# A patch-and-text transformer block on one core: stationary values, 32-row score tiles, a mask written by TensorE, and a nine-step pipe in attention

## The chip, the cores and the metric

One core of one Trainium2 chip runs the whole program. The metric is device time in microseconds (us), lower is better; the median of a few runs is compared. The core has five instruction queues: PE (TensorE, matrix products), DVE (VectorE), ACT (ScalarE), POOL (GpSimd) and SP (SyncE, which here only issues DMAs). Each runs its own instructions in program order, and they wait for each other through semaphores.

## What is computed

```python
h = tok(x)                             # 32 x 36 patches of 768: layernorm, @ Wp + bp, layernorm
h = concatenate([h, txt], axis=1)      # 32 sequences of T = 113 rows, D = 256
h = h + attn(layernorm(h))
h = h + ffn(layernorm(h))              # blockwise FP4 of inputs and weights, SwiGLU, inner width 704
# attn(x):
q = (x @ Wq.T).reshape(B, T, 16, 16); k = (x @ Wk.T).reshape(B, T, 16, 16)
v = (x @ Wv.T).reshape(B, T, 8, 32)
q = rotary(rmsnorm(q)) / 4; k = rotary(rmsnorm(k))      # per head of 16
attn = softmax(where(causal, q @ k.T, -inf))            # 16 score heads
attn = attn[:, :, 0] - lam * attn[:, :, 1]              # pairs of them
out = layernorm(attn @ v) * (1 - LAMBDA_INIT)           # per head of 32
return out.reshape(B, T, 256) @ Wproj.T
```

## The kernel before

The program has three stages. The front makes the patch tokens, nine tiles of 128 rows (`front(i)`), quantises the weights of the last stage piece by piece and prepares the attention weights; it writes tokens to `h_dram`. The attention stage works on one sequence at a time: `attention(b)` is one pass of a software pipe, in which each engine does different steps of several sequences (the number ahead of a step in the lists called `steps` is added to b: `(2, qk)` makes the queries and keys of sequence b + 2). The feed-forward stage (FFN) works on 29 tiles of 128 rows. All three are written for five engines at once by `pipeline`, which interleaves the last front steps with the first passes and the last passes with the first FFN steps; the middle passes are a hardware loop. The order on each engine is written by hand; only semaphores tie the engines.

What one pass does, for the sequences in flight: SP loads the rows `hx` (two DMAs, patch rows and text rows), DVE takes their moments (`ln_sums`), ACT takes Ln and Exp of all variances of the pass together (`roots`, tile `var`), DVE refines them (`newton_step`) and normalises (`ln_apply`, tile `xn`). PE transposes, ACT and DVE split the result into a high and a low half (`xo_hi`, `xo_lo`), and PE multiplies by the weights in three products (`split3`, line L138). `scale_qk`, `cosines`, `sines` (on POOL) and `rope_sum` apply the norm and the rotation; the four tiles of that are all called `rope` in the trace. PE transposes them; ACT writes the keys (`k_t`) and the queries in blocks (`q_blk`), of which four slots share 64 rows. PE makes four groups of scores, ACT exponentiates each, POOL zeroes the later keys in each (`mask`), and PE multiplies: the probabilities are the stationary operand, the values with a column of ones (33 columns) the moving one, once for each of 16 heads. DVE mixes the pairs (`mix`: L931 to L942), and another norm, the transposes, the output product (`project`) and the residual (L967, with rows loaded again as `hr`) follow. Stores go to `h2_dram`. `bank_a` holds both the transposes (`xo_ps`) and the output product, so the transposes of the next pass wait for the residual.

```python
def residual(b):
    dve.wait_ge(m["proj_made"], b - 1)
    dve.wait_ge(m["hr_loaded"], 32 * b - 32)
...
run(b, seq, (
    (3, ln_sums), (-1, mix), (1, rope_sum), (-2, residual),
    (2, qk_sums), (-1, z_sums), (-2, out_sums), (-1, z_var), (2, qk_var),
    ((3, -2), variances)))
```

## Time and profile before

| | |
|---|---|
| time, median of 3 runs | 660.13 us (658.75 to 660.4) |
| time of the profiled execution | 662.52 us |
| its span | 660.8 us |
| PE busy | 576.4 us (87%) |
| DVE busy | 554.1 us (84%) |
| ACT busy | 322.1 us (49%) |
| POOL busy | 309.8 us (47%) |
| granted TensorE clock, mean | 0.948 |

The span runs from the first to the last instruction. A busy share is an average over three stages, so it says little by itself; what a pass of the loop costs is read from the timelines of the engines. A mean of one of the costliest groups (L741, the product with the values) is 262 ns for each of 1024 instructions, but matmuls overlap, so their cost is read from the distance between starts.

### The profile page before, as it was taken

What the parts mean: (1) busy time and instruction counts of PE and PEld (TensorE: products, weight loads), DVE (VectorE), ACT (ScalarE), POOL (GpSimd) and SP (SyncE); (2) the same over time, 40 slices, a digit from 0 to 9 for tenths busy, and PEclk for the clock granted to TensorE, in tenths of its full rate; (3) what the DMA queues carried; (4) which work ended last, traced back from release to release, by engine and by line L of the source; (5) the groups of instructions that cost most, each with busy time, mean ns of one, the idle gap of its engine ahead of it and who ended that gap; (6) DMA issues with size and microseconds to landing.
All of it is one profiled execution on the core that took longest, in us unless ns stands there. A gap on an engine that the chain in (4) does not pass through costs nothing. (4 is left out here: it accounts for less than half of the span.)

```text
span 660.8 us, 14226 instructions
## 1 busy us (share of the span) xinstructions
PE 576.4 (87%) x3666; PEld 470.0 (71%) x3666; DVE 554.1 (84%) x1444; ACT 322.1 (49%) x760; POOL 309.8 (47%) x455
## 2 busy tenths in 40 slices
PE   5665568999999999999999998589999999999996
PEld 4554455767776776777677676478888888888885
DVE  5999847898889889888988985498888888888884
ACT  2242215655665665566565564244544444445442
POOL 2455523555455445545554553155455445545542
PEclk9878776999999999999999997789999999999999
DMA  6900000011111111111111101111111111111111
GB/s 173 325 17 23 24 16 18 27 38 41 30 40 35 35 35 38 40 34 37 35 41 29 42 23 46 30 39 49 48 54 52 54 48 54 49 48 48 57 32 35
DMA packets 33734, 31.99 MB, mean 48 GB/s; under 512 B 6098, under 2 KB 32050, under 8 KB 33714
## 3 DMA queue, kind: packets, MB, share of 16 engines
q1 hardware_dynamic: 33714, 31.75, 16.3%
q8 instruction: 9, 0.15, 0.1%
q14 instruction: 11, 0.09, 0.0%
HBM read 23.02 MB, written 8.71 MB: 48 GB/s over the span
## 5 line engine op out<-in xcount | busy, mean ns | idle before, releaser
L741 PE MATMUL bank<-v_sb,pt 113*113 113x33 f32 x1024 | 109.1, 262 | 0.0
L741 PEld LDWEIGHTS bank<-v_sb,pt 113*113 113x113 f32 x1024 | 108.4, 181 | 0.7 <-issue 0.7
L858 POOL TENSOR_SCALAR_AFFINE_SELECT pt<-pt 113x452 f32<-113x452 f32 x128 | 73.9, 600 | 68.5 <-ACT pt L798 68.5
L798 ACT ACTIVATE pt<-bank 113x452 f32<-113x452 f32 x128 | 63.1, 545 | 38.2 <-PE bank L729 38.2
L138 PE MATMUL bank<-wgu_hi,fx_hi 128*128 128x512 f32 x174 | 69.5, 399 | 8.0 <-DVE fx_lo L1131 8.0
L1177 POOL TENSOR_TENSOR h_deq<-fh,fhb 128x704 f32<-128x704 f32 x29 | 40.3, 1389 | 68.8 <-DVE fhb L1084 56.3
L729 PE MATMUL bank<-q_blk,k_t 64*113 64x452 f32 x256 | 67.7, 605 | 0.0
L138 PE MATMUL bank<-wgu_hi,fx_lo 128*128 128x512 f32 x174 | 66.8, 384 | 0.0
L138 PE MATMUL bank<-wgu_lo,fx_hi 128*128 128x512 f32 x174 | 66.7, 384 | 0.0
L138 PE MATMUL bank<-wqkv_hi,xo_hi 128*113 128x256 f32 (+1 forms) x128 | 50.3, 393 | 17.7 <-DVE xo_lo L923 17.7
L1191 POOL TENSOR_TENSOR fh<-fh,fhb 128x704 f32<-128x704 f32 x29 | 40.3, 1391 | 42.2 <-DVE fhb L1145 42.2
L138 PE MATMUL bank_a<-wd_hi,fh_hi 128*128 128x256 f32 x174 | 54.4, 313 | 2.4 <-DVE fh_lo L1088 2.4
L138 PEld LDWEIGHTS bank<-wqkv_hi,xo_hi 128*113 128x113 f32 x128 | 23.5, 183 | 43.0 <-issue 34.2
L867 POOL COPY v_sb<-v_next 113x256 f32<-113x256 f32 x32 | 12.8, 401 | 87.0 <-PE bank L741 63.8
L850 POOL TENSOR_TENSOR rope<-rope,trig 113x256 f32<-113x256 f32 x64 | 46.4, 744 | 13.1 <-DVE rope L905 13.1
L138 PE MATMUL bank_a<-wd_lo,fh_hi 128*128 128x256 f32 x174 | 49.1, 282 | 0.0
L138 PE MATMUL bank_a<-wd_hi,fh_lo 128*128 128x256 f32 x174 | 49.0, 282 | 0.0
L1243 ACT ACTIVATE bank_b<-fx 128x256 fp32r<-128x256 f32 x29 | 11.3, 388 | 76.2 <-POOL fx L1184 75.1
L809 ACT ACTIVATE q_blk<-bank_b,slot_rows 128x226 f32<-128x226 f32 x128 | 46.4, 445 | 0.0
L138 PE MATMUL bank<-wqkv_lo,xo_hi 128*113 128x256 f32 (+1 forms) x128 | 45.0, 352 | 0.0
L138 PE MATMUL bank<-wqkv_hi,xo_lo 128*113 128x256 f32 (+1 forms) x128 | 44.7, 350 | 0.0
L138 PEld LDWEIGHTS bank<-wgu_hi,fx_hi 128*128 128x128 f32 x174 | 33.8, 194 | 14.2 <-DVE fx_lo L1131 5.6
(160 smaller groups left out, 1531.3 us busy)
## 6 DMA issues: line engine op xcount, KB each, us to landing
xb<-h_dram SPq DMA_DIRECT2D x29, 129.0 KB, 2.1
rb<-h_dram SPq DMA_DIRECT2D x29, 128.0 KB, 2.0
h_dram<-h SPq DMA_DIRECT2D x32, 112.9 KB
out<-res SPq DMA_DIRECT2D x28, 128.0 KB, 1.7
px<-in_patches SPq DMA_DIRECT2D x9, 384.0 KB, 10.1
hx<-in_txt SPq DMA_DIRECT2D x32, 77.0 KB
hr<-in_txt SPq DMA_DIRECT2D x32, 77.0 KB
wf<-in_wgu SPq DMA_DIRECT2D x1, 1408.0 KB, 8.0
```

What stands on the lines that cost most here:

```text
L138: last = pe.matmul(dst, a(k), w(k), start=(start and n == 0), stop=(n == len(passes) - 1))
L729: pe.matmul(sc_ps[g % 2][0:T, :], k_t[rows, c, :], q_blk[rows, c, :, :].rearrange("p s t -> p (s t)"), start=True, stop=True).then_inc(m[" ...
L741: mm = pe.matmul(pv_ps[s % 2][0:T, s // 2, :], pt[0:T, s, :], v_sb[0:T, s // 2, :], start=True, stop=True, skip_group_check=True)
L798: act.activation(pt[0:T, GS * g:GS * (g + 1), :].rearrange("p s t -> p (s t)"), sc_ps[g % 2][0:T, :], ACT.Exp, scale=1.0 / math.sqrt(HD)). ...
L809: i = act.activation(q_blk[:, :, s, :], qkt_ps[:, 0:KD, :], ACT.Copy, scale=slot_rows[:, s:s + 1])
L850: pool.tensor_tensor(dst[:, :, half, :], src[:, :, 1 - half, :], table, ALU.mult).then_inc(m["qk_sin"], 1)
L858: pool.affine_select(out=grp, in_=grp, compare_op=ALU.is_ge, fill=0.0, base=0, pattern=[[0, GS], [1, T]], channel_multiplier=-1).then_inc( ...
L867: pool.tensor_copy(v_sb[0:T, :, 0:VD], blocks(v_next[0:T, :], VD)).then_inc(m["v_moved"], 1)
L1177: pool.tensor_tensor(blocks(h_deq[:, 0:INTER], BLK), blocks(h_code[:], BLK), spread(h_scale[:], BLK), ALU.mult).then_inc(f["h_deq"], 1)
L1191: pool.tensor_tensor(blocks(h_quot[:], BLK), blocks(hid[:], BLK), spread(h_inv[:], BLK), ALU.mult).then_inc(f["h_quot"], 1)
L1243: act.activation(x_abs.bitcast(F32R), x_quot[:], ACT.Abs, scale=STEP).then_inc(f["x_abs"], 1)
```

## The change

- Scores: a tile has 32 rows (two slots) in place of 64, so four tiles lie one under the other; each has its own bank. `scores` writes the causal mask into each bank first (identity times a table of 0 and -32768, both bfloat16), and eight products of 226 columns add to it. POOL's `mask` is gone.
- Values: `pv` keeps a head's values stationary (32 columns) and moves the probabilities of the pair (226 columns), four heads at four column positions. The result is transposed, so ACT copies it (`ot_copy`) and PE turns it back (`pv_transposes`). A rotation of each head's values by a zero-sum basis, made in the front, leaves 31 columns; the 32nd carries the sum of the probabilities. It also carries the epsilon of the norm of the output, so `eps0` and `z_var` are gone.
- Norm: the attention weights are centred in the front (`turn_values`, `average_attention`, `turn_projection` on PE, `centre_attention` and `attn_low` on DVE), so `hx` is transposed as it is, `ln_apply` is gone, the values take the norm's factor in `v_stage`, and the rmsnorm takes it as its epsilon (`epsilons`, POOL).
- `rope_sum` moves from DVE to POOL.
- The pipe has nine steps: passes -4 to 35 in place of -3 to 34. The residual is three passes behind (`(-3, residual)`), the store four; `xo_hi`, `xo_lo`, `rstd` and `v_sb` have two buffers; the loop body holds two passes.

```diff
-ROW = P // 2
+ROW = P // NG
...
+MASKED = -2.0 ** 15
...
+            def centre_attention(_):
+                dve.wait_ge(k["wqkv_averaged"], 1)
+                for cols, mean in ((slice(0, 2 * D), bank_a[:]), (slice(2 * D, 3 * D), bank_b[:, 0:D])):
+                    w = wqkv_raw[:, :, cols]
+                    dve.tensor_tensor(w, w, mean.unsqueeze(1).broadcast_to(list(w.shape)),
+                                      ALU.subtract).then_inc(k["wqkv_centred"], 1)
...
-            def v_subtract(_):
...
-            def attn_low(c):
-                pool.wait_ge(k["attn_high"], 2)
-                pool.tensor_tensor(wqkv_lo[:, c, :], wqkv_raw[:, c, :], wqkv_hi[:, c, :].bitcast(F32),
-                                   ALU.subtract).then_inc(k["attn_low"], 1)
...
+            def turn_values(_):
...
+            def average_attention(_):
+                pe.wait_ge(k["wv_copied"], 1)
+                pe.wait_ge(k["bias_ready"], 1)
+                for cols, mean in ((slice(0, 2 * D), bank_a[:]), (slice(2 * D, 3 * D), bank_b[:, 0:D])):
+                    for c in range(KD):
+                        mm = pe.matmul(mean, average_d[:], wqkv_raw[:, c, cols], start=(c == 0), stop=(c == KD - 1))
+                mm.then_inc(k["wqkv_averaged"], 1)
+            def turn_projection(_):
...
-                if seq(b, 3):
-                    after(sp, m["ln_applied"], b + 3)
-                    load_rows(hx, b + 3, m["hx_loaded"])
-                if seq(b, -3):
-                    sp.wait_ge(m["h2_ready"], b - 2)
-                    sp.dma_start(h2_dram[bass.ds((b - 3) * T, T - 1), :], h2[0:T - 1, :]).then_inc(m["h2_stored"], 16)
-                    sp.dma_start(h2_dram[bass.ds((b - 3) * T + T - 1, 1), :], h2[T - 1:T, :]).then_inc(m["h2_stored"], 16)
-                if seq(b, -1):
-                    after(sp, m["h2_added"], b - 1)
-                    load_rows(hr, b - 1, m["hr_loaded"])
...
+            def load(s, _):
...
+                after(sp, m["ln_stats"], s)
+                after(sp, m["xo_made"], s)
+                load_rows(sp, hx, s, m["hx_loaded"])
+            def load_residual(s, _):
+                after(sp, m["h2_added"], s)
+                load_rows(sp, hr, s, m["hr_loaded"])
...
+                run_order(b, odd, one, ((-4, store), (-2, load_residual), (4, load)))
...
-            def transposes(b):
-                after(pe, m["h2_added"], b - 2)
-                if seq(b, 2):
-                    pe.wait_ge(m["ln_applied"], b + 3)
-                    for k in range(KD):
...
+            def transposes(s, odd):
+                after(pe, m["h2_added"], s - OD)
+                after(pe, m["xo_low"], s)
...
-            def scores(b, g):
...
+            def scores(s, odd):
...
+                pe.wait_ge(m["q_blocked"], s + 1)
+                pe.wait_ge(m["kt_copied"], s + 1)
+                after(pe, m["exp_made"], NG * s)
+                after(pe, m["ot_copied"], s)
+                for r in range(NG):
+                    pe.matmul(sc_ps[r][0:T, :], ident_16[0:T, 0:T], mask_16[0:T, :], start=True, stop=True)
+                for c in range(KD):
+                    for r in range(NG):
+                        rows = slice(r * ROW, (r + 1) * ROW)
+                        mm = pe.matmul(sc_ps[r][0:T, c * SLOTS * T:(c + 1) * SLOTS * T], k_t[rows, c, :],
+                                       q_blk[rows, c, :, :].rearrange("p s t -> p (s t)"),
+                                       start=False, stop=True, skip_group_check=True)
+                        if c == KD - 1:
+                            mm.then_inc(m["scores_made"], 1)
...
+            def pv(s, odd):
+                pe.wait_ge(m["exp_made"], NG * s + NG)
+                pe.wait_ge(m["v_staged"], s + 1)
+                for c in range(KD):
+                    for r in range(NG):
+                        mm = pe.matmul(ot_ps[r * VD:(r + 1) * VD, c, :, :].rearrange("p s t -> p (s t)"),
+                                       v_sb[odd][0:T, c * NG + r, :],
+                                       pt[0:T, r, c * SLOTS:(c + 1) * SLOTS, :].rearrange("p s t -> p (s t)"),
+                                       start=True, stop=True, skip_group_check=True)
...
+            def pv_transposes(s, odd):
+                pe.wait_ge(m["ot_copied"], s + 1)
+                after(pe, m["mix_step"], 4 * s)
+                after(pe, m["v_staged"], min(NSEQ, s + 3) if isinstance(s, int) else s + 3)
+                for i in range(2):
+                    for c in range(KD):
+                        mm = pe.transpose(o_ps[0:T, i, c, :], ot_sb[:, c, i, :], ident[:])
+                mm.then_inc(m["pv_back"], 1)
...
-                run(b, seq, (
-                    ((2, -2), transposes), (0, scores, 0), (0, scores, 1), (2, qk), (-2, project)))
...
-                    (0, scores, 2), (0, scores, 3), (1, qk_transposes), (0, pv, 0), (0, pv, 1), (2, v),
-                    (0, pv, 2), (0, pv, 3)))
+            def steps(b, odd):
+                run_order(b, odd, exists, (
+                    (-3, project), (0, scores), (-1, pv_transposes), (2, qk), (0, pv), (3, transposes),
+                    (1, qk_transposes), (2, v)))
...
+            def roots(s, odd):
+                after(act, m["newton"], 3 * (s + LD))
+                if one(s):
+                    act.wait_ge(m["qk_sums"], s + 1)
+                if one(s - ZD):
+                    act.wait_ge(m["z_sums"], s - ZD + 1)
+                if one(s + LD):
+                    act.wait_ge(m["ln_var"], s + LD + 1)
+                if one(s - UD):
+                    act.wait_ge(m["out_var"], s - UD + 1)
...
+            def ot_copy(s, odd):
+                act.wait_ge(m["pv_made"], s + 1)
+                after(act, m["pv_back"], s)
+                act.activation(ot_sb[:], ot_ps, ACT.Copy).then_inc(m["ot_copied"], 1)
...
-                run(b, seq, (((2, -2), xo_high),))
-                if between:
-                    between()
-                run(b, seq, (
-                    (0, exps, 0), (0, exps, 1), (1, v_stage), (2, squares),
-                    (-1, z_square), (0, exps, 2), (0, exps, 3), (1, k_copy), ((3, -2), roots),
-                    (1, q_blocks)))
...
+            def v_stage(s, odd):
...
+                act.wait_ge(m["newton"], 3 * s + 3)
...
+                run_order(b, odd, exists, (
+                    (0, exps, 0), (0, exps, 1), (0, exps, 2), (0, exps, 3), (2, squares), (-1, z_square),
+                    (0, ot_copy), (3, xo_high), (1, k_copy), (1, q_blocks), (2, roots), (2, v_stage)))
...
+            def epsilons(s, odd):
+                pool.wait_ge(m["ln_var"], s + 1)
+                after(pool, m["qk_sums"], s)
...
+                pool.tensor_scalar(sq[0:T, :, HD], var[0:T, 0:1].broadcast_to([T, 2 * SH]), RMS_EPS, None,
+                                   ALU.mult).then_inc(m["eps_set"], 1)
...
-            def mask(b, g):
...
+            def rope_sum(s, odd):
+                pool.wait_ge(m["qk_cos"], s + 1)
+                pool.wait_ge(m["qk_sin"], 2 * s + 2)
+                after(pool, m["qkt_made"], s)
+                pool.tensor_tensor(qkr[0:T, :], qkc[0:T, :], qks[0:T, :], ALU.add).then_inc(m["qk_roped"], 1)
...
+                run_order(b, odd, some, (
+                    (2, epsilons), (-4, join_moments), (1, sines), (1, rope_sum)))
...
-            def ln_apply(b):
...
-                    ((2, -3), newton_step), (2, ln_apply), (-2, o_apply), (1, scale_qk), (1, cosines),
-                    ((2, -2), xo_low)))
...
-                    (3, ln_sums), (-1, mix), (1, rope_sum), (-2, residual),
-                    (2, qk_sums), (-1, z_sums), (-2, out_sums), (-1, z_var), (2, qk_var),
-                    ((3, -2), variances)))
...
+                run_order(b, odd, exists, (
+                    (3, ln_sums), (1, newton_step), (1, scale_qk), (-2, o_apply), (1, cosines), (-1, ratios),
+                    (-1, mix_product), (-1, mix_sum), (-3, residual), (2, qk_sums), (-3, out_sums),
+                    (-1, z_sums), (3, xo_low), (-3, out_variance), (3, ln_variance)))
...
-            for i in range(-1, PT - 3):
+            for i in range(-1, PT - 5):
                 front(i)
-            attention(-3)
-            front(PT - 3)
-            attention(-2, lambda: front(PT - 2))
-            attention(-1, lambda: front(PT - 1))
-            attention(0, lambda: front(PT))
-            for b in range(1, 4):
-                attention(b)
-            with engine.Fori(4, NSEQ - 3) as b:
-                attention(b)
+            for b in range(FIRST, LOOP[0]):
+                if b < 2:
+                    front(PT - 1 + b)
+                attention(b, b % 2)
+            with engine.Fori(LOOP[0], LOOP[1] - 1, step=2) as b:
+                attention(b, 0)
+                attention(b + 1, 1)
```

SyncE, one pass just ahead of the loop. `hx` are the rows of the sequence that enters, `hr` those of the residual, `h` the result. Before:

```order
L663 DMA hx<-h_dram 36x256 [waits a_ln_applied]
L664 DMA hx<-in_txt 77x256
L679 DMA h_dram<-h 112x258 [waits a_h2_ready]
L680 DMA h_dram<-h 1x258
L663 DMA hr<-h_dram 36x256 [waits a_h2_added]
L664 DMA hr<-in_txt 77x256
```

After:

```order
L759 DMA h_dram<-h 112x258 [waits a_h2_ready]
L760 DMA h_dram<-h 1x258
L737 DMA hr<-h_dram 36x256 [waits a_h2_added]
L738 DMA hr<-in_txt 77x256
L737 DMA hx<-h_dram 36x256 [waits a_xo_made,a_ln_stats]
L738 DMA hx<-in_txt 77x256
```

The load of `hx` stood first, behind `ln_applied`; it now stands last, behind the load of `hr`, which waits for the residual's sum (`a_h2_added`).

VectorE, one pass from its roots on (`var` and `rstd` are variances and factors, `mix` and `mix_o` tiles of the output norm, `bank_a` the transposes or the output product). Before:

```order
L888 TENSOR_TENSOR var<-var 113x42 [waits a_root_made]
L890 SCALAR_TENSOR_TENSOR var<-var 113x42 [waits a_newton]
L892 SCALAR_TENSOR_TENSOR var<-var 113x42 [waits a_newton]
L896 TENSOR_SCALAR xn<-hx,moments,var 113x256 [waits a_newton]
L901 SCALAR_TENSOR_TENSOR mix<-mix,var 113x256
L905 TENSOR_TENSOR rope<-bank,var 113x512
L910 TENSOR_TENSOR rope<-rope,trig 113x512 [waits a_qk_scaled]
L923 TENSOR_TENSOR xo_lo<-bank_a,xo_hi 128x452 [waits a_xo_high]
L975 BN_STATS st_in<-hx 113x6 [waits a_hx_loaded]
```

After:

```order
L1090 BN_STATS st_in<-hx 113x6 [waits a_hx_loaded]
L1004 TENSOR_TENSOR var<-var 113x42 [waits a_v_staged,a_root_made]
L1006 SCALAR_TENSOR_TENSOR var<-var 113x42 [waits a_newton]
L1008 SCALAR_TENSOR_TENSOR rstd<-var 113x42 [waits a_newton]
L1014 TENSOR_TENSOR rope<-bank,rstd 113x512 [waits a_qk_sin,a_qk_cos,a_newton]
L1028 SCALAR_TENSOR_TENSOR mix_o<-mix,rstd 113x256 [waits a_xo_made,a_newton]
L1020 TENSOR_TENSOR rope<-rope,trig 113x512 [waits a_qk_roped,a_qk_scaled]
L1043 RECIPROCAL sum<-bank 113x8 [waits a_pv_back]
L1045 SCALAR_TENSOR_TENSOR sum<-bank,lam,sum 113x8 [waits a_mix_step]
L1050 TENSOR_TENSOR mix<-bank,sum 113x8x31 [waits a_mix_step]
L1056 TENSOR_TENSOR mix<-bank,mix 113x256 [waits a_z_squared,a_mix_step]
L1074 TENSOR_TENSOR h<-bank_a,hr 113x256 [waits a_h2_stored,a_hr_loaded,a_proj_made]
```

The statistics of the loaded rows (`st_in<-hx`) stood behind the roots and `xo_lo`; they now open the pass. `xn` is gone, and `xo_lo` stands behind the residual (`h<-bank_a,hr`).

GpSimd, one pass. Before:

```order
L839 TENSOR_SCALAR h<-moments,var 113x1 [waits a_newton]
L840 COPY h<-var 113x1
L850 TENSOR_TENSOR rope<-rope,trig 113x32x8 [waits a_qk_roped,a_qk_scaled]
L850 TENSOR_TENSOR rope<-rope,trig 113x32x8
L858 AFFINE_SELECT pt<-pt 113x452 [waits a_exp_made] x4
L867 COPY v_sb<-v_next 113x8x32 [waits a_v_staged,a_pv_made]
```

After:

```order
L956 TENSOR_SCALAR sq<-var 113x32 [waits a_ln_var,a_qk_sums]
L964 TENSOR_SCALAR h<-moments,rstd 113x1 [waits a_newton]
L965 COPY h<-rstd 113x1
L975 TENSOR_TENSOR rope<-rope,trig 113x32x8 [waits a_qk_roped,a_qk_scaled]
L975 TENSOR_TENSOR rope<-rope,trig 113x32x8
L983 TENSOR_TENSOR rope<-rope 113x512 [waits a_qkt_made,a_qk_sin,a_qk_cos]
```

The four masks and the copy of the values are gone; the sum of the two rotated halves (`rope<-rope` of 512) stands behind the sines.

## Rows read from the trace of the kernel before

**Rows 1.** Windows by stage: busy time of each engine, then granted clock.

```profile
205.00:285.00 80.00, 75.36 (x560) 58.84 (x558) 70.99 (x211) 48.46 (x127) 39.00 (x74) 1.00 0.12 36
```

**Rows 2.** Timeline of VectorE, one pass of the attention loop (start, duration).

```profile
198.25 0.20 DVE L888 TENSOR_TENSOR var<-var 113x42 f32<-113x42 f32 x1 [0.58 <-ACT var L780]
...
198.96 0.41 DVE L896 TENSOR_SCALAR xn<-hx,moments,var 113x256 f32<-113x256 f32 x1
199.29 0.42 DVE L901 SCALAR_TENSOR_TENSOR mix<-mix,var 113x256 f32<-113x256 f32 x1
199.63 0.68 DVE L905 TENSOR_TENSOR rope<-bank,var 113x512 f32<-113x512 f32 x1
200.34 0.80 DVE L910 TENSOR_TENSOR rope<-rope,trig 113x512 f32<-113x512 f32 x1
201.22 0.63 DVE L923 TENSOR_TENSOR xo_lo<-bank_a,xo_hi 128x452 fp32r<-128x452 f32 x1
201.93 0.43 DVE L975 BATCH_NORM_STATS2 st_in<-hx 113x6 f32<-113x256 f32 x1
202.27 0.19 DVE L931 RECIPROCAL sum<-bank 113x8 f32<-113x8 f32 x1
...
202.71 0.62 DVE L936 SCALAR_TENSOR_TENSOR sum<-sum 113x8 f32<-113x8 f32 x1
...
204.04 0.68 DVE L918 TENSOR_TENSOR rope<-rope 113x512 f32<-113x512 f32 x1
204.64 0.42 DVE L967 TENSOR_TENSOR h<-bank_a,hr 113x256 f32<-113x256 f32 x1
...
207.85 0.20 DVE L888 TENSOR_TENSOR var<-var 113x42 f32<-113x42 f32 x1 [0.58 <-ACT var L780]
```

**Rows 3.** Line L888, the first operation of a pass on VectorE.

```profile
L888 DVE TENSOR_TENSOR var<-var x26: 203/205/205, 140.6 to 380.6; 113x42 f32<-113x42 f32 x26
```

**Rows 4.** Timeline of SyncE's DMA issues in the same pass.

```profile
199.56 0.30 SPq L663 DMA_DIRECT2D hx<-h_dram  x1
200.06 0.30 SPq L664 DMA_DIRECT2D hx<-in_txt  x1
...
205.24 0.33 SPq L663 DMA_DIRECT2D hr<-h_dram  x1
205.76 0.32 SPq L664 DMA_DIRECT2D hr<-in_txt  x1
```

**Rows 5.** Timeline of GpSimd in the same pass.

```profile
201.36 1.40 POOL L850 TENSOR_TENSOR rope<-rope,trig 113x256 f32<-113x256 f32 x2
202.72 1.14 POOL L858 TENSOR_SCALAR_AFFINE_SELECT pt<-pt 113x452 f32<-113x452 f32 x2
```

**Rows 6.** Timeline of VectorE later, GpSimd idle: L936 again.

```profile
402.55 0.16 DVE L936 SCALAR_TENSOR_TENSOR sum<-sum 113x8 f32<-113x8 f32 x1
```

**Rows 7.** Timeline of TensorE in an early pass of the loop.

```profile
126.90 0.28 PE L138 MATMUL bank_a<-wproj_hi,xo_hi 128*113 128x256 f32 x1
...
127.69 1.02 PE L729 MATMUL bank<-q_blk,k_t 64*113 64x452 f32 x4
128.64 0.61 PE L756 MATMUL bank_b<-ident,rope 113*128 113x113 f32 x4
129.08 1.68 PE L741 MATMUL bank<-v_sb,pt 113*113 113x33 f32 x16
130.60 0.35 PE L138 MATMUL bank<-wqkv_hi,xo_hi 128*113 128x256 f32 x1
```

**Rows 8.** Timeline of ScalarE in the pass of rows 2.

```profile
201.52 0.99 ACT L798 ACTIVATE pt<-bank 113x452 f32<-113x452 f32 x2 [0.34 <-PE bank L729]
```

**Rows 9.** Timeline of VectorE in the start-up stage.

```profile
56.56 1.73 DVE L384 SCALAR_TENSOR_TENSOR t<-t 128x2 f32<-128x2 f32 x1
```

**Rows 10.** Timeline of GpSimd in the start-up stage.

```profile
38.18 1.06 POOL L578 TENSOR_TENSOR wn<-wf,wblk 128x512 f32<-128x512 f32 x1 [2.07 <-DVE wblk L438]
...
56.46 1.80 POOL L597 TENSOR_TENSOR wqkv_lo<-wqkv_raw,wqkv_hi 128x768 fp32r<-128x768 f32 x1
```

531 lines of the change are left out of this document (274 added, 257 removed).

## The prediction

> **What bounds the kernel now.** I read the windows by stage first. In the middle of the attention loop, 80 us hold 75.4 us of TensorE, 71.0 of VectorE, 48.5 of ScalarE and 39.0 of GpSimd, at the full clock [rows 1]: two engines are nearly full and neither is quite the bound by its share. Then the period: line L888 opens a pass on VectorE, and its 26 starts from 140.6 to 380.6 us make 25 passes of 9.60 us, 240 of the 660.8 us [rows 3]. The timeline of VectorE inside one pass tells the rest: from 198.25 to 207.85 it has one idle stretch, 0.58 us, while ScalarE makes the roots [rows 2]. So the pass is VectorE's own 9.0 us of work plus the one hop that closes its ring. TensorE, with 9.04 us a pass (75.36 / 80 x 9.60), stands just behind. A gain must come from both.
>
> **TensorE, step by step.** A pair of score tiles takes 0.95 us to the next start (127.69 to 128.64), twice a pass: 1.90. Half of the products with the values take 1.52 (129.08 to 130.60), so 3.04 a pass [rows 7]. Both go: 9.04 - 4.94 = 4.10. The score pair also shows that tiles in different rows overlap: four instructions (two for each product) of 452 columns in 0.95 us. Eight products of 226 columns, four tiles at a time, are 0.95 us if four overlap as two do; one after another they are at most 16 x 0.95 / 4 = 3.8. The same bounds hold for `pv`, whose tiles lie side by side in columns; no row shows such tiles. I take 0.95 for each, as the one overlap that is shown is clean. Four mask products are not in the trace; by 452 columns of the score rows one instruction is at least 0.95 / 4 = 0.24 and at most twice that, and I take 0.2 each, 0.8, since they have a single pass and no partner (low bound; high 1.9). `pv_transposes` are four like those of the rotated tile, 0.44 (128.64 to 129.08) [rows 7]. Sum: 4.10 + 0.95 + 0.95 + 0.8 + 0.44 = 7.24 us.
>
> The Trainium skill (TensorEngine Tiling (Array Packing), "Performance Considerations" and "Key Properties") gives up to four times for 32 rows or 32 columns, and a drain at each change of mode; TensorE: Matmul & The Clock Gate, Part 3, measures 3.07 times for four row tiles and 2.38 for three column tiles. By it the two stages would be some 1.0 to 1.3 us each, an estimate of the pages, and the sum some 0.5 higher. No run here shows four tiles yet.
>
> **VectorE.** Gone: `ln_apply` 0.33 (198.96 to 199.29), `rope_sum` 0.60 (204.04 to 204.64), L936 about 0.55 of its 0.62, and three small ones, `s0`, `z_var` and `qk_var`, for which I take 0.6 together (between 0.3, twice L936's undisturbed 0.16, and 1.1) [rows 2, 6]. New: one more small sum, 0.2. 9.0 - 2.1 + 0.2 = 7.1, and the root hop of 0.58, part of which `ln_sums` (0.34) now covers: 7.3 to 7.7 us.
>
> ScalarE, at 5.8 us a pass (48.46 / 80 x 9.60), loses two of four query blocks and gains a copy of 452 columns, about as long as one exponential, 0.55 (0.99 for two, the second starting at 0.44): below 6.4 in any case [rows 1, 8]. GpSimd loses four masks (0.57 each) and gets 512 elements of `rope_sum`, 1.06 by a product of that size [rows 5, 10]. Neither binds.
>
> **The ring that I think binds.** Two things stand in a new order. On SyncE the load of `hx` is last, behind that of `hr`, and `hr` waits for the residual's sum of the same pass. On VectorE `ln_sums` opens the pass, so all of it waits for that load. Followed round: residual done; 0.19 to SyncE's issue (as from 199.37 to 199.56); three issues at 0.52, two for `hr` and the first for `hx` (205.24 to 205.76), 1.56; from the second issue of `hx` to the statistics 1.87 (200.06 to 201.93) [rows 2, 4]: 3.62. Then on VectorE, to the next start each: `ln_sums` 0.34 (201.93 to 202.27), `newton_step` 0.71 (198.25 to 198.96), `scale_qk` 0.71 (199.63 to 200.34), `o_apply` 0.34 (199.29 to 199.63), `cosines` 0.60 (as L918, same shape), the mix 1.25 (202.27 to 204.04 less L936's share of 0.54), the residual 0.42 [rows 2]: 4.37. The ring is **8.0 us** when nothing disturbs it. What VectorE does between the residual and the next roots (two sums, two statistics, `xo_lo`, the variances: some 2.6 at the 0.3 to 0.6 that such rows take) and the hop of 0.58 are 3.2, and fit beside the 3.62; the load is the longer branch by 0.4, and by 0.8 with `ln_sums`.
>
> What disturbs it is GpSimd. L936, 113x8, took 0.62 us from 202.71, to the very end of a mask that started at 202.72 (two in 1.14, so the first to 203.3), and 0.16 when GpSimd was idle [rows 2, 5, 6]. `o_apply` and `cosines` read two SBUF tensors, as L936 does, and now stand right where GpSimd runs `join_moments` and the sines, 0.70 each [rows 5]. A wait of one sine half less the fill that overlaps it is 0.6; the bounds are 0 (VectorE first) and 1.3 (both halves). I take 0.6: **8.6 us** a pass.
>
> The Trainium skill (SBUF — State Buffer, "SBUF: two separate sides") says why: VectorE and GpSimd share a port pair, an exclusive lock for the whole instruction, taken by a VectorE operation with two SBUF inputs against a GpSimd one that reads SBUF. By that rule, against the change in that it puts more VectorE operations beside sines, a pass is 8.6; without it 8.0. The trace agrees with the rule at L936.
>
> **The ends.** Start-up: front step 3 gets TensorE products (centring and turning, some 12 passes of 256 to 512 columns at a partly low clock) on which VectorE waits, then two subtractions of 1024 and 512 elements and `attn_low` there; by 0.68 for 512 elements [rows 2] that is 2.0 + 2.0, and 2 to 4 us of waiting. Against it GpSimd no longer does 2 x 1.80 of `attn_low`, behind which a 128x2 operation stood for 1.73 us [rows 9, 10], and that twice or more. I take +3 (bounds -2 and +7). The pipe's two extra passes lie beside front and FFN steps that are there anyway: 0 (if that cover were missing, two nearly empty passes, some 3 us each). Some six passes beside the loop have attention nearly in full; I give them 0.8 us of gain each: -5. The FFN's code does not change: 0.
>
> **Sum.** 24 passes with a load x (9.60 - 8.6) = -24; ends -5 + 3 = -2. Span 660.8 - 26 = 634.8. The profiled execution took 662.5, 1.7 over its span and 2.4 over the median of the runs, so I forecast **634 us** (660.1 - 26).
>
> **Rivals.**
> 1. The load ring without disturbance, or shorter: passes of 7.6 to 8.2, where VectorE or the TensorE-ScalarE ring sets the pace: `xo_lo` 0.6 (452 elements, near L918's 0.60 for 512) [rows 2], `project` 0.79, masks and scores 1.75, four exponentials 3 x 0.44 + 0.55 = 1.87, `pv` 1.0, two copies 1.05, five hops of some 0.1: 7.6 [rows 7, 8]. For it: cosines may win the port. Savings of 1.4 to 2.0 in 24 passes and the same ends: 660.1 - 2 - 34 to 48, so 610 to 624 us.
> 2. Four tiles overlap worse than pairs do, and a wait for TensorE sets the pace: 1.4 to 1.8 us more in scores and `pv` bring the ring of rival 1 to 9.0 to 9.4 us, 0.2 to 0.6 saved: 642 to 655. For it: no row has four tiles; against it: the pairs overlap cleanly.
> 3. Slower: the column tiles of `pv` run one after another. The ring above, which holds `pv` whole since the copies wait for it, is then 7.6 + 2.85 = 10.45 us, +0.85 x 25 - 2 = some 680 us. It decides from 1.9 us more than I took in `pv` and the scores together (9.6 - 7.6). Against it: row tiles do overlap; for it: no row shows column tiles.
> 4. The reordering brings nothing, because a wait of the same length replaces the work (a ring of 9.5 to 9.6 by two full sine waits and longer DMA): 657 to 662.
>
> **Chances.** Main case (8.3 to 8.9 us a pass, 624 to 642) 0.42; rival 1 0.28; rival 2 0.15; rival 3 0.10; rival 4 0.05. The time is that of the main case; the range of 8 in 10 reaches from rival 1 into rival 2: 611 to 655. Within 0.3% is about what this measurement can tell from no change: 2 us. Faster 0.86 (main, rival 1 and all but a little of rival 2), same 0.03, slower 0.11.
>
> **What would show it.** Right: passes of 8.6 us in the loop, VectorE idle ahead of the statistics of `hx` with a DMA as releaser, the `hx` issues right behind those of `hr`, `cosines` longer than 0.69 and ending with a sine; scores and `pv` about 1 us each. Wrong: VectorE idle ahead of the root or `xo_lo` instead (rival 1 or 2), `pv` of some 3.8 us (rival 3), or a gap of over 5 us in the front.

## The result, and the profile after

Medians of four runs each: before 659.79 us (658.75 to 660.4), after **630.29 us** (626.41 to 631.72), a ratio of 0.9545 with a 95% interval of 0.9498 to 0.9592. That is 29.5 us less; the forecast was 634.

A pass of the loop takes 8.65 us on average (VectorE's L1004 starts at 237.99 and, eight passes on, at 307.20), 9.60 before [rows 3]. The windows of the same 80 us of the loop as in [rows 1] (busy time of each engine, then the granted clock):

```profile
205.00:285.00 80.00, 70.06 (x616) 48.55 (x616) 66.02 (x186) 52.51 (x130) 37.34 (x57) 1.00 0.14 41
```

TensorE's 70.06 of 80 us are 7.58 us a pass, VectorE's 66.02 are 7.14. Both have more than a microsecond of room now, so neither is the bound by its own work. The timeline of VectorE in one pass, to be read against [rows 2]:

```profile
220.40 0.43 DVE L1090 BATCH_NORM_STATS2 st_in<-hx 113x6 f32<-113x256 f32 x1 [1.03 <-DMA hx<-in_txt]
...
221.57 0.69 DVE L1014 TENSOR_TENSOR rope<-bank,rstd 113x512 f32<-113x512 f32 x1 [0.17 <-DVE rstd L1008]
222.18 0.41 DVE L1028 SCALAR_TENSOR_TENSOR mix_o<-mix,rstd 113x256 f32<-113x256 f32 x1
222.51 1.22 DVE L1020 TENSOR_TENSOR rope<-rope,trig 113x512 f32<-113x512 f32 x1
...
224.94 0.41 DVE L1074 TENSOR_TENSOR h<-bank_a,hr 113x256 f32<-113x256 f32 x1
...
226.70 0.63 DVE L1035 TENSOR_TENSOR xo_lo<-bank_a,xo_hi 128x452 fp32r<-128x452 f32 x1
...
227.83 0.15 DVE L1099 TENSOR_SCALAR var<-moments 113x1 f32<-113x1 f32 x1
229.09 0.43 DVE L1090 BATCH_NORM_STATS2 st_in<-hx 113x6 f32<-113x256 f32 x1 [1.11 <-DMA hx<-in_txt]
```

The pass opens with an idle stretch of 1.0 to 1.1 us, which the landing of `hx` ends, where before the roots ended one of 0.58. Over the whole kernel this wait is 28.4 us in 28 times (view of line L1090, its idle time by releaser):

```profile
  DMA hx<-in_txt: 28.4, 28
```

SyncE's issues in that pass, against [rows 4]:

```profile
225.52 0.33 SPq L737 DMA_DIRECT2D hr<-h_dram  x1
226.04 0.32 SPq L738 DMA_DIRECT2D hr<-in_txt  x1
226.68 0.30 SPq L737 DMA_DIRECT2D hx<-h_dram  x1
227.17 0.30 SPq L738 DMA_DIRECT2D hx<-in_txt  x1
```

The residual ends at 225.35; 0.17 later the two `hr` issues begin, the two of `hx` come right behind them, and 1.92 us after the last one (227.17) the statistics start (229.09). GpSimd in the same pass (the two sines, then the sum):

```profile
222.35 1.97 POOL L975 TENSOR_TENSOR rope<-rope,trig 113x256 f32<-113x256 f32 x2 [0.35 <-DVE rope L1014]
224.40 1.27 POOL L983 TENSOR_TENSOR rope<-rope 113x512 f32<-113x512 f32 x1
```

The first sine starts at 222.35, 0.16 ahead of the cosines. These take 1.22 us where the same multiplication takes 0.69 alone (e1 below), and the two sines together 1.97 in place of 1.42. TensorE in the next pass:

```profile
228.18 0.93 PE L814 MATMUL bank<-mask,ident 113*113 113x452 bf16 x4
229.04 1.04 PE L818 MATMUL bank<-q_blk,k_t 32*113 32x226 f32 x16
230.01 0.69 PE L843 MATMUL bank<-ident,ot_sb 128*113 128x128 f32 x4
231.05 0.45 PE L152 MATMUL bank<-wqkv_hi,xo_hi 128*113 128x512 f32 x1 [0.35 <-DVE rope L1014]
...
232.59 0.97 PE L830 MATMUL bank<-pt,v_sb 113*32 113x226 f32 x16
```

To the next start the masks take 0.86 us and the scores 0.97. The row of the product with the values (`pv`) lasts 0.97 itself; the next start comes later, since TensorE then waits 0.56 for the residual. In e3 below, where nothing is waited for behind it, the next start is 0.90 and 1.00 us away in two passes (216.71 to 217.61, 224.49 to 225.49).

**Where the time went, by stretches of the two traces.** I cut both at the first operation of the Newton step in passes b = 4 and b = 29. Up to b = 4: 140.6 before [rows 3], 125.2 after, so 15.4 less. None of it lies ahead of the first Newton step, that of b = -2, which starts at 74.45 before and at 76.00 after; the six passes from there to b = 4 take 66.1 and 49.2 us. From b = 4 to 29: 240.0 and 215.7, so 24.3 less. From b = 29 to the end of the span: 280.2 (660.8 - 380.6) and 283.8 (624.7 - 340.9), so 3.6 more; the traces of e5, e9 and e10 below, whose tail is the same, have 284.5, 283.2 and 286.6, so the loss is 3 to 6 us. Together the spans differ by 36.1 us. The medians differ by 29.5, because the profiled execution of before lies 2.7 above its median (662.5) and that of after 3.9 below (626.4).

The tail's loss stands between the first two tiles of the FFN: L1222, which makes `hidden`, starts at 383.51 and 399.40, 15.9 us apart where before they were 7.8 apart (429.76 and 437.56). ScalarE (rows of table loads) and VectorE there:

```profile
392.93 1.28 ACT L882 ACT_TABLE_LOAD   x1 [7.18 <-DVE var L1086]
...
394.48 1.28 ACT L884 ACT_TABLE_LOAD   x1
...
396.71 1.28 ACT L1322 ACT_TABLE_LOAD   x1
```

```profile
391.44 0.42 DVE L1074 TENSOR_TENSOR h<-bank_a,hr 113x256 f32<-113x256 f32 x1 [2.86 <-DMA h_dram<-h]
...
396.73 0.89 DVE L1190 SCALAR_TENSOR_TENSOR fh<-h_abs,fh 128x704 f32<-128x704 bf16 x1 [3.87 <-ACT h_abs L1315]
...
399.40 0.83 DVE L1222 TENSOR_TENSOR fh<-bank,fh 128x704 f32<-128x704 f32 x1
```

The pipe is one pass longer, so the last roots come behind the first silu. Before, ScalarE has one table load in this stretch, at 427.68 behind the last roots; after, it has four, one at 381.42 and the three shown, which load the tables for Ln, Exp and Silu again, 1.28 us each. VectorE's FFN step waits 3.87 us behind them. Ahead of that, the last residual waits 2.86 us for the store of the `h2` before it.

The start-up's gain, in the windows from 75 to 105 us, before and then after:

```profile
75.00:105.00 30.00, 19.47 (x68) 14.87 (x68) 17.03 (x51) 7.38 (x23) 6.23 (x9) 0.67 0.05 17
```

```profile
75.00:105.00 30.00, 24.30 (x146) 17.61 (x145) 21.64 (x67) 14.29 (x41) 14.35 (x19) 0.89 0.09 26
```

TensorE's instructions in these 30 us are 146 in place of 68, and the granted clock is 0.89 in place of 0.67. What was waited for, in the view of waits from 60 to 104 us (us in total, times, longest; L408 and L451 are VectorE's steps on the token product, before and after), before:

```profile
DVE y L408 <- PE bank L641: 8.8, 2, 5.1
...
PE bank_a L696 <- DVE xn L896: 6.1, 2, 3.9
```

and after:

```profile
DVE y L451 <- PE bank L715: 0.9, 1, 0.9
```

Before, TensorE stood 6.1 us for the normalised `xn`, and VectorE 8.8 us for the token product that stands behind those transposes in TensorE's order. After, that line of VectorE waits 0.9. Two larger waits of this view shrank as well, and no experiment took them apart: ScalarE for VectorE's `t` (19.0 us before, 10.5 after) and TensorE for GpSimd's `wn` (10.6 and 8.4).

### The profile page after: what moved, and what is told of

The parts are those of the page before. It is cut to its first block and busy times, and to the rows that moved or that the text cites. A ratio compares the mean times of both kernels' runs of the same rounds, so it can differ in the third digit from the quotient of the medians.

```text
span 624.7 us, 13838 instructions
## 1 busy us (share of the span) xinstructions
PE 523.6 (84%) x3686; PEld 412.6 (66%) x3686; DVE 505.2 (81%) x1288; ACT 322.5 (52%) x735; POOL 278.1 (45%) x357
## 5 line engine op out<-in xcount | busy, mean ns | idle before, releaser
L904 ACT ACTIVATE pt<-bank 113x452 f32<-113x452 f32 x128 | 59.7, 553 | 32.9 <-PE bank L818 32.9
L975 POOL TENSOR_TENSOR rope<-rope,trig 113x256 f32<-113x256 f32 x64 | 62.0, 988 | 20.2 <-DVE rope L1014 20.2
L152 PE MATMUL bank<-wqkv_hi,xo_hi 128*113 128x256 f32 (+1 forms) x128 | 48.6, 380 | 11.4 <-DVE rope L1014 11.4
L1190 DVE SCALAR_TENSOR_TENSOR fh<-h_abs,fh 128x704 f32<-128x704 bf16 x29 | 25.9, 892 | 21.0 <-ACT h_abs L1315 21.0
L983 POOL TENSOR_TENSOR rope<-rope 113x512 f32<-113x512 f32 x32 | 40.8, 1275 | 3.1
L956 POOL TENSOR_SCALAR sq<-var 113x32 f32<-113x32 f32 x32 | 10.2, 318 | 69.5 <-DVE var L1099 69.5
L1393 PE MATMUL bank<-ident,h_deq 128*128 128x128 f32 x174 | 25.8, 286 | 15.8 <-POOL h_deq L1272 15.7
L152 PEld LDWEIGHTS bank<-wgu_lo,fx_hi 128*128 128x128 f32 x174 | 34.0, 196 | 5.6
L1020 DVE TENSOR_TENSOR rope<-rope,trig 113x512 f32<-113x512 f32 x32 | 37.5, 1172 | 0.1
L152 PEld LDWEIGHTS bank<-wgu_hi,fx_lo 128*128 128x128 f32 x174 | 33.8, 194 | 5.7
```

The costliest lines, as they stand in the source:

```text
L152: last = pe.matmul(dst, a(k), w(k), start=(start and n == 0), stop=(n == len(passes) - 1))
L904: act.activation(pt[0:T, r, :, :].rearrange("p s t -> p (s t)"), sc_ps[r][0:T, :], ACT.Exp, scale=1.0 / math.sqrt(HD)).then_inc(m["exp_mad ...
L956: pool.tensor_scalar(sq[0:T, :, HD], var[0:T, 0:1].broadcast_to([T, 2 * SH]), RMS_EPS, None, ALU.mult).then_inc(m["eps_set"], 1)
L975: pool.tensor_tensor(dst[:, :, half, :], src[:, :, 1 - half, :], table, ALU.mult).then_inc(m["qk_sin"], 1)
L983: pool.tensor_tensor(qkr[0:T, :], qkc[0:T, :], qks[0:T, :], ALU.add).then_inc(m["qk_roped"], 1)
L1020: dve.tensor_tensor(blocks(qkc[0:T, :], HD), blocks(qkn[0:T, :], HD), trig[0:T, 0, :].unsqueeze(1).broadcast_to([T, 2 * SH, HD]), ALU.mult ...
```

## The experiments

All are edits of the changed kernel, timed beside the kernel before.

| kernel | median us (range) | ratio to before, 95% interval | pass us |
|---|---|---|---|
| changed kernel | 630.3 (626.4 to 631.7) | 0.9545 (0.9498 to 0.9592) | 8.65 |
| e1, cosines first | 617.4 (614.7 to 619.9) | 0.9368 (0.9331 to 0.9405) | 8.08 |
| e2, late statistics | 619.2 (618.6 to 621.2) | 0.9393 (0.9367 to 0.9419) | 8.31 |
| e3, both | 611.5 (608.7 to 612.9) | 0.9260 (0.9225 to 0.9295) | 7.95 |
| e4, hx first | 621.3 (618.2 to 624.2) | 0.9429 (0.9395 to 0.9464) | 8.35 |
| e5, wait in front | 627.1 (626.1 to 631.0) | 0.9517 (0.9471 to 0.9564) | |
| e6, tail | 623.9 (621.9 to 624.6) | 0.9441 (0.9404 to 0.9479) | |
| e7, loops exchanged | 629.1 (one run) | | |
| e8, e3 and e6 | 609.3 (605.7 to 611.0) | 0.9222 (0.9172 to 0.9271) | 7.95 |
| e9, transposes first, wait | 635.6 (635.1 to 636.0) | 0.9607 (0.9560 to 0.9654) | |
| e10, transposes first | 632.2 (628.4 to 633.6) | 0.9540 (0.9481 to 0.9598) | |
| e11, e8 and two h2 | 604.9 (603.9 to 605.8) | 0.9145 (0.9098 to 0.9191) | 7.96 |
| e12, one tile | 811.0 (one run) | | |

**The ring of the loop: e1 to e4.**

```diff
# e1, GpSimd, sines
-                pool.wait_ge(m["qk_scaled"], s + 1)
+                pool.wait_ge(m["qk_cos"], s + 1)
# e2, VectorE's order
-                    (3, ln_sums), (1, newton_step), (1, scale_qk), (-2, o_apply), (1, cosines), (-1, ratios),
+                    (1, newton_step), (1, scale_qk), (-2, o_apply), (1, cosines), (-1, ratios),
...
-                    (-1, z_sums), (3, xo_low), (-3, out_variance), (3, ln_variance)))
+                    (-1, z_sums), (3, ln_sums), (3, xo_low), (-3, out_variance), (3, ln_variance)))
# e4, SyncE's order
-                run_order(b, odd, one, ((-4, store), (-2, load_residual), (4, load)))
+                run_order(b, odd, one, ((-4, store), (4, load), (-2, load_residual)))
```

e1: 

> Changed kernel with one wait moved: GpSimd's sines of a sequence wait for VectorE's cosines of it. Theory A (the pass of 8.65 us is the ring residual, hr issues, hx issues, landing, VectorE's work up to the next residual, and the cosines stand in it with 0.5 us of sine behind which they wait): cosines 0.69 instead of 1.22 us, a pass of about 8.15 us, 24 x 0.5 = 12 us less, near 618 us. Theory B (the pace is set by TensorE and ScalarE, and VectorE's wait for hx only fills what is left): cosines shorter, the wait for hx longer by the same 0.5 us, 630 us as now. Theory C (the rope chain decides: cosines, sines, sum, transposes): the sines end 0.7 us later, a pass of 8.8 to 9.0 us, 634 to 640 us.

Measured: 617.4 us and 8.08 us a pass. VectorE and GpSimd in a pass of e1:

```profile
221.86 0.43 DVE L1090 BATCH_NORM_STATS2 st_in<-hx 113x6 f32<-113x256 f32 x1 [1.08 <-DMA hx<-in_txt]
...
223.93 0.69 DVE L1020 TENSOR_TENSOR rope<-rope,trig 113x512 f32<-113x512 f32 x1
224.53 0.20 DVE L1043 RECIPROCAL sum<-bank 113x8 f32<-113x8 f32 x1
```

```profile
224.78 1.42 POOL L975 TENSOR_TENSOR rope<-rope,trig 113x256 f32<-113x256 f32 x2 [1.32 <-DVE rope L1020]
226.28 1.27 POOL L983 TENSOR_TENSOR rope<-rope 113x512 f32<-113x512 f32 x1
```

The cosines are back at 0.69, the two sines take 1.42, and the wait for `hx` is still there with 1.08 us. It did not grow by what the cosines lost, as theory B had it: the whole pass became shorter by 0.57. So the cosines stand inside the ring. The sines start later, and the pass did not grow by it: theory C falls.

e2: 

> Changed kernel with the statistics of hx moved on VectorE from the start of the pass to behind z_sums. Theory A: nothing else on VectorE waits for the load, so the ring through DMA is open by some 4 us; what is left is VectorE's 7.1 us of work with the root hop of 0.6 to 0.9 us uncovered, a pass of 7.8 to 8.1 us, 24 x 0.55 to 0.85 less: 610 to 617 us. Theory B (TensorE and ScalarE set the pace): 8.65 us a pass and 630 us, with another wait on VectorE in the place of the one on hx.

Measured: 619.2 us, 8.31 us a pass, both just outside what theory A gave (610 to 617 us, 7.8 to 8.1 a pass) and far from B. VectorE in a pass of e2:

```profile
223.05 0.42 DVE L1090 BATCH_NORM_STATS2 st_in<-hx 113x6 f32<-113x256 f32 x1
...
224.49 0.15 DVE L1099 TENSOR_SCALAR var<-moments 113x1 f32<-113x1 f32 x1
225.62 0.20 DVE L1004 TENSOR_TENSOR var<-var 113x42 f32<-113x42 f32 x1 [0.98 <-ACT var L884]
```

The wait for `hx` is gone and the statistics (223.05) start with no idle time; what ends VectorE's idle stretch now is the root, 0.98 us. That hop was 0.58 before [rows 2], and `ln_sums` had covered a part of it. The work (67.21 of 80 us, at 8.31 us 7.0 a pass) and this hop leave 0.3 us for small gaps. The ring through DMA was the bound, and taking it away gives 0.34 us, because the next ring, VectorE's own with the root in it, is only that much shorter while the cosines still wait for a sine.

e3: 

> Both edits of e1 and e2. Theory A: the pass falls to TensorE's own 7.6 us (70.06 of 80 us busy at 8.65 us a pass) or little over it, 7.6 to 7.8, some 605 to 610 us; less than the two savings together, because another ring takes over. Theory B: 630 us. If only the lock mattered, e3 is as e1.

Measured: 611.5 us and 7.95 us a pass; 0.70 saved where the two alone saved 0.57 and 0.34. The windows of e3 in the loop, and two rows of its waits in those 80 us:

```profile
205.00:285.00 80.00, 75.28 (x668) 52.19 (x665) 65.58 (x201) 57.16 (x142) 33.98 (x60) 1.00 0.16 44
```

```profile
DVE var L1004 <- ACT var L884: 10.0, 11, 1.0
...
PE bank_b L859 <- POOL rope L983: 4.6, 10, 0.6
```

TensorE's 75.28 of 80 us are 7.48 a pass, and it waits about 0.5 us a pass for the sum on GpSimd, while VectorE waits 1.0 for the root. I had given 7.6 to 7.8 and left out the rope chain. Passes alternate between 7.7 and 8.2 us (starts 237.19, 244.91, 253.07, 260.79); why they do is open.

e4: 

> Changed kernel with SyncE's loads of hx issued ahead of those of hr. Theory A: the hx load then waits for the transposes of the pass instead of for two hr issues; these end some 0.9 us behind the residual, so the hx issues come 0.3 to 0.5 us earlier than now, a pass of 8.15 to 8.35 us, 620 us. Theory B: 630 us. If the wait for hr then grows (its issue is 1 us later), the residual waits for it, and the time is 630 us or over.

Measured: 621.3 us and 8.35 us a pass, both as theory A gave them. The wait for `hx` is shorter by 0.3 us, in the row of 225.71:

```profile
223.63 0.63 DVE L1035 TENSOR_TENSOR xo_lo<-bank_a,xo_hi 128x452 fp32r<-128x452 f32 x1
...
225.71 0.43 DVE L1090 BATCH_NORM_STATS2 st_in<-hx 113x6 f32<-113x256 f32 x1 [0.80 <-DMA hx<-in_txt]
```

Three edits at three places of one ring (the stall of an operation in it, the operation at its head, the order of its issues) each shortened the pass, e1 and e4 by the amount forecast, e2 by less (0.34 us against 0.55 to 0.85); theory B expected no change in any.

**Tiles of TensorE: e7 and e12.**

```diff
# e7, scores, and pv in the same way
-                for c in range(KD):
-                    for r in range(NG):
+                for r in range(NG):
+                    for c in range(KD):
# e12, scores: all products on the same rows; pv: eight more products ahead, all in the same columns
-                        rows = slice(r * ROW, (r + 1) * ROW)
+                        rows = slice(0, ROW)
...
+                        pe.matmul(ot_ps[0:VD, c, :, :].rearrange("p s t -> p (s t)"),
+                                  v_sb[odd][0:T, c * NG + r, :],
...
```

e7: 

> Changed kernel with the two loops of scores and of pv exchanged: both chunks of a tile directly behind each other, so that neighbouring products mostly use the same rows (scores) or the same columns (pv). If tiles overlap as the rows of 0.97 us say and only between different tiles, a stage of eight products of two instructions becomes 1.4 to 1.9 us, scores and pv alike, and the pass grows from 8.65 to 8.8 to 9.6 us (TensorE has 1.1 us of room), 634 to 653 us. If the order doesn't matter (the 0.97 us is the rate at which 16 instructions of 226 columns go through anyway), 0.97 us stays and so do 630 us.

Measured: one run, 629.1 us; scores and pv 0.99 us each where they were 0.97 (220.67 to 221.66 in its trace, and 224.16). In this one run the order of the two loops is worth 0.02 us a stage. It does not tell whether tiles overlap; e12 does.

e12: 

> Changed kernel with all eight score products on the same 32 rows (rows 0 to 31 of k_t and q_blk, so that the scores are other numbers), and with eight more pv products ahead of the eight there are, all eight in the same 32 columns. Theory (0.97 us a stage is four tiles at work at once): the scores take 3 to 3.9 us in place of 0.97, and pv 0.97 plus 3 to 3.9 us, the pass some 4 to 6 us longer, 730 to 780 us. Rival (0.97 us is only the rate of sixteen instructions of 226 columns, wherever they stand): scores 0.97, pv 1.94 us, the pass at most 1 us longer, 630 to 650 us.

Measured: one run, 811.0 us. The scores in a pass of e12:

```profile
312.76 3.31 PE L818 MATMUL bank<-q_blk,k_t 32*113 32x226 f32 x16
316.00 0.69 PE L849 MATMUL bank<-ident,ot_sb 128*113 128x128 f32 x4
```

They take 3.24 us to the next start, where the kernel with four row tiles takes 0.97: a factor of 3.3. The pass before, from the first of the sixteen products with the values to the next stage:

```profile
305.18 3.05 PE L830 MATMUL bank<-pt,v_sb 113*32 113x226 f32 x15
307.88 0.39 PE L836 MATMUL bank<-pt,v_sb 113*32 113x226 f32 x3
308.07 0.35 PE L830 MATMUL bank<-pt,v_sb 113*32 113x226 f32 x1
308.10 1.09 PE L836 MATMUL bank<-pt,v_sb 113*32 113x226 f32 x13
309.12 0.41 PE L777 MATMUL bank_a<-ident,hx 113*128 113x113 f32 x2
```

Both eights took 3.94 us (305.18 to 309.12); less 0.97 for those on four tiles, the eight in one column tile took 3.0, a factor of 3.1. The granted clock was 1.00 in both stretches (305.0 to 309.2 and 312.0 to 316.1), so it has no part in the factors. For the rows the eight products still went to four banks as before, and only the rows changed. For the columns one rival stays: four products each also wrote to the same place of the result, and no run has that without the shared columns. So 0.97 us is the work of tiles side by side, shown for rows and, but for that rival, for columns; and by e7 the two products of one tile may stand back to back. Over 80 us of the loop (205 to 285) the granted clock was 0.89 in this run, so its total time holds more than the longer stages, and it lies above the 730 to 780 us expected; the rival's 630 to 650 is far off.

**The start-up: e5, e9, e10.**

```diff
# e5 (and, up to s = 4, e9), transposes on TensorE
+                    if isinstance(s, int) and s <= 5:
+                        after(pe, m["newton"], 3 * s)
# e9 and e10, TensorE's order while b <= 1
-                    (-3, project), (0, scores), (-1, pv_transposes), (2, qk), (0, pv), (3, transposes),
+                        (3, transposes), (-3, project), (0, scores), (-1, pv_transposes), (2, qk), (0, pv),
```

e5: 

> Changed kernel, but in the start-up passes (sequences 1 to 5) the transposes on TensorE wait for the Newton step of their own pass, as those of before waited for ln_apply behind it. Theory F (the start-up gained because the transposes now take raw hx: before, TensorE stood 6.1 us at them and the token product behind them in its order made VectorE wait 8.8 us in two pieces, at its line L408; after, 0.9 us): that wait comes back, the start-up is 5 to 12 us longer, 635 to 642 us. Theory G (it gained by GpSimd's masks and attn_low, or by VectorE's lighter passes): 630 us, as now.

Measured: 627.1 us; from b = -2 to b = 4 49.0 us (75.90 to 124.94), in the changed kernel 49.2 (76.00 to 125.23), before 66.1 (74.45 to 140.57). Theory F as put there falls: the wait alone costs nothing, since at its place behind `pv` the Newton step has long been done (TensorE waits 0.2 us for it in all, from 60 to 104 us).

e9: 

> Changed kernel, but in the start-up passes up to b = 1 TensorE's transposes stand first in the pass, as in before, and wait for the Newton step of their own pass. e5 had the wait alone, behind pv, and cost nothing. Theory H (what the start-up gained is the pair of both: a transpose that heads TensorE's pass and waits for VectorE holds up all that stands behind it, the next token product too): b = 4 at 133 to 142 us in place of 125.2, 637 to 646 us. Theory G (neither matters; the start-up is shorter for the work that was taken off VectorE and GpSimd): 630 us.

e10: 

> As e9, but without the wait for the Newton step: the transposes head the pass and take raw hx. Theory H: 628 to 632 us, since it needs both. If the place alone is what counts (the copies on ScalarE and xo_lo behind it come at another time), as e9.

Measured: e9 635.6 us, with 59.9 us from b = -2 to 4 (75.13 to 135.06); e10 632.2 us, with 51.0 (78.29 to 129.26). e9's TensorE waits for the Newton step again:

```profile
PE bank_a L779 <- DVE rstd L1015: 6.5, 3, 2.5
```

```profile
75.00:105.00 30.00, 22.21 (x113) 15.86 (x114) 15.96 (x48) 9.85 (x28) 11.51 (x15) 0.79 0.07 21
```

Theory H gave b = 4 at 133 to 142 and 637 to 646 us; the first came true, the second is missed by 1.4. How much this stretch varies by itself is told by e6 below, whose start-up code is that of the changed kernel: 50.7 us (78.14 to 128.87), where the changed kernel's own trace has 49.2. So place and wait together bring back 9.2 to 10.7 of the 16.9 us, and the place alone (51.0) nothing that stands clear of that spread. By the medians e9 is only 5.3 us over the changed kernel (4 by the ratios), so the size rests on one trace.

From 105 to 125 us the granted clock is 0.83 in e9 and 0.85 before, and 1.00 in the changed kernel, e5, e6, e7 and e10; what that costs by itself was not measured.

Yet the wait did not come back where I had seen it: VectorE's wait for the token product stays under 1 us in e9, and the time stands in other rows (TensorE for the Newton step 6.5, ScalarE for the q and k product 9.1 where the changed kernel has 6.1). The other 6.2 to 7.7 us are open. Neither the work taken off GpSimd and VectorE nor the new place of the front's last steps, which now lie between the passes -4 to 1 instead of inside -2 to 0, was tried by itself.

**The tail: e6, e8, e11.**

```diff
# e6, on all engines but TensorE
                 attention(b, b % 2)
-                if b >= NSEQ - EARLY and not (tile_first and b == NSEQ + 1):
+                if b == NSEQ + 2 and not tile_first:
+                    ffn(0)
+                if b >= NSEQ - EARLY and b != NSEQ + 1:
                     ffn(b - NSEQ + EARLY - 3)
# e11 beside that (and two places for its moments), two h2 buffers, one semaphore for the stores of each
-                after(dve, m["h2_stored"], 32 * s)
+                after(dve, h2_stored[odd], 16 * (s - odd))
```

e6: 

> Changed kernel, but on VectorE, ScalarE, GpSimd and SyncE the FFN's step 0 stands behind attention pass 34 in place of behind pass 33, so that all roots are made before the first silu; TensorE's order is unchanged. Theory T (the tail lost some 8 us since the last roots come behind the first silu, with two more table loads of 1.28 us each and a queue of waits round them): 4 to 8 us less, 622 to 626 us, one load of the silu table, FFN tiles 0 and 1 some 8 us apart in place of 15.9. Theory U (what bounds there is the last residual and its store, whatever stands around them): the first hidden comes 6 to 8 us later, the second where it is now, 628 to 632 us.

Measured: 623.9 us. ScalarE has one table load there:

```profile
387.96 0.24 ACT L884 ACTIVATE var<-var 113x42 f32<-113x42 f32 x1
388.21 1.28 ACT L1319 ACT_TABLE_LOAD   x1
```

The changed kernel has four. By medians that is 6.4 us less, inside what theory T gave. The trace doesn't bear this size out: `hidden` of tile 0 starts at 390.30 and of tile 1 at 398.57, against 383.51 and 399.40, which is what theory U said of the two tiles, and counted from b = 29 (342.59 and 340.89) the last `hidden` (606.8 and 607.6) comes 2.5 us sooner. e5, timed together with e6 and alike in the tail, has 627.1, 3.1 us more by the medians and 5 by the ratios. I put e6 at 2.5 to 3 us, by the traces and these medians; up to 5 is not excluded. T and U both have a part: the three extra table loads go, but most of the 8 us between the two tiles is not won by that.

e8: 

> Edits of e1, e2 and e6 together. Theory T: 4 to 8 us under e3's 611.5 us, 604 to 607 us. Theory U: 611 us. No interaction is expected, since e3 shortens the loop and e6 the tail.

Measured: 609.3 us, 2.2 under e3, whose interval it overlaps; it fits 2.5 and neither forecast.

e11: 

> e8 (cosines first, late statistics of hx, FFN's step 0 behind pass 34) with two h2 buffers and two places for their moments, so that the residual of a sequence waits for the store before last. In the tail the residual of the last pass waits 2.8 us for the store of the one before (e6's VectorE at 386.18 us), and in the loop 0.1 us a pass. Theory: 2 to 5 us under e8's 609.3 us, 604 to 607 us. Rival: the tail's chain is newton, roots and projection and the store only comes last by a little: 609 us.

Measured: **604.9 us**, a ratio of 0.9145 (0.9098 to 0.9191), the fastest of all and 25 us under the changed kernel. By the ratios it is 5 us under e8, the upper end of the forecast 2 to 5; the two intervals only just overlap. In e8 the residual still waited for stores:

```profile
  DMA h_dram<-h: 5.3, 4
```

In e11 no such wait is left at that line, and the last Newton step starts at 381.75 in place of 386.39. So in the last passes the store of one `h2` held up the next residual, where no other work covers it.

## Why the prediction was right, point by point

**The loop.** Forecast 8.6 us a pass by the ring residual, `hr` issues, `hx` issues, landing, VectorE; measured 8.65. Residual to issue 0.17 (0.19 forecast), issues 1.65 from the first to the last (1.56), landing 1.92 (1.87), VectorE from the statistics to the residual's end 4.95 (220.40 to 225.35; 4.37 + 0.6), in it the cosines' 1.22 in place of 0.69 (0.6 for the stall, 0.53 measured). One of these terms came right by luck. The 1.87 was read as a landing, but before the change VectorE never waited for `hx`: the view of line L975 has these 26 executions with no idle time ahead of any.

```profile
L975 DVE BATCH_NORM_STATS2 st_in<-hx x26: 417/427/429, 125.3 to 365.0; 113x6 f32<-113x256 f32 x26
```

So the row gave only an upper bound for the landing. e1, e2 and e4 show the ring by breaking it at three places. Rival 1 (7.6 to 8.2 a pass) was the wrong account of this kernel; it is what e1 and e3 measure once the disturbance is gone.

The rule cited in the prediction (the Trainium skill, SBUF — State Buffer, "SBUF: two separate sides") was held against the change, and the trace agrees with it: the first sine starts 0.16 us ahead of the cosines, and these end 1.22 us after their start, which is their own 0.69 and the 0.53 left of one sine of 0.7. The page also says that whichever operation starts first gets the pair; the sine, which started first, ran on, and the second one then waited for the cosines (the pair took 1.97 in place of 1.42). In e1 the two engines no longer meet there: the sines start when the cosines are done.

**TensorE.** Forecast 7.24 us a pass, measured 7.58 (7.48 in e3). Scores 0.95 forecast, 0.97 measured, pv 0.95 and 0.90 to 1.00, masks 0.8 and 0.86, `pv_transposes` 0.44 and 0.59 (222.36 to 222.95 in e3). Rival 2 (tiles overlap worse than pairs) and rival 3 (column tiles one after another, `pv` of some 3.8 us) fall with these rows; e12 measures what a serial stage costs here, 3.24 us for the rows and 3.0 for the columns, so rival 3's 3.8 us was a quarter too high and its condition did not hold. The speedups cited there (the Trainium skill, TensorEngine Tiling (Array Packing) and TensorE: Matmul & The Clock Gate, Part 3) are 3.07 times for four row tiles and 2.38 for three column tiles, of 512 columns each; here, with 226 columns, e12 against the changed kernel gives 3.3 for four row tiles and 3.1 for four column tiles.

**VectorE.** Forecast 7.1 us of work, taken as the pass less its marked idle time (9.60 - 0.58 = 9.0 before). By the same measure the pass from 220.40 to 229.09 has 8.69 - 1.11 = 7.58, in which the cosines' stall of 0.53 is counted; without it 7.05, as forecast. (The busy sums of the windows, 7.14 with the stall and 8.52 before, leave out small gaps, and are not comparable with the 7.1.) The root hop is 0.98 us (e2), not 0.58.

**Start-up: the step that failed most.** The front itself, "+3 (bounds -2 and +7)", was not it: the first Newton step came 1.6 us later (76.00 for 74.45; with the same front at 74.7 to 78.3 in the experiments). What failed is the term behind it, "some six passes beside the loop have attention nearly in full; I give them 0.8 us of gain each: -5". The six passes from b = -2 to 4 alone gained 16.9 us, 2.8 each. I priced them as lighter passes of the loop, and not what TensorE's new order takes away where front and attention share the engines. The 8.8 us of waiting at L408 and the granted clock of 0.67 stood in the trace and were not used. e9 shows that place and wait of the transposes carry 9.2 to 10.7 us of it; the rest is open.

**The pipe's extra passes: forecast 0,** and with the lighter passes beside the loop some -2 to -3 in the tail; measured +3.6 from b = 29 on (3 to 6 over four traces). The cover that I named (FFN steps that are there anyway) holds for the work, and not for the table loads nor for the store that the last residual waits for. e6 and e11 give back 2.5 to 3 and about 5 us. The condition named with that zero, two nearly empty passes of 3 us each, is of the size of this loss, but its cause is another.

The forecast of 634 is thus near 630.3 by a right loop (-24 forecast, -24.3 measured), and in part by luck. The ends were forecast at -2 together and measured at -15.4 and +3.6, so -11.8: 9.8 us missed, which the opposite signs made smaller. Of the 36.1 us by which the two profiled spans differ, the medians show 29.5, since the profiled run of before was slower than its median and that of after the fastest of its four; these 6.6 us brought the result back towards the forecast's -26.

## What to carry to other kernels

When a change puts a load at the head of an engine's pass, walk the ring from the buffer's release through the DMA queue back to it, with each issue ahead of it in the queue: four issues some 0.5 us apart and a landing of 1.9 us were 3.6 of the 8.65 us of this loop's ring, and moving one operation out of it was worth 11 us. Of two operations of VectorE and GpSimd that compete, let the one on the ring go first: here one wait on another semaphore gave 13 us. Read a start-up and a tail for what heads the order of each engine there; this pipe, made deeper, paid at its end, in table loads and in a store that the loop's other work covers.
